# Attention's output projection moved into the steps, token selection into the last step, heavy path among light units

## What is computed

```python
q, k, v   = split((xn @ W_qkv + b_qkv).reshape(B, 16 heads, 1024, 48))
attention = softmax(q k^T * scale + causal mask) @ v, reshaped, @ W_out + b_out
light     = gelu(rms(xn) * gamma_l @ w1_l + b1_l) @ w2_l + b2_l        # hidden 128, all tokens
a, b      = 50 iterations of coordinate descent on s = xn @ routing_token
heavy     = for the 256 tokens of each batch with the largest exp((s + a + b) / 0.1):
            gelu(rms(xn) * gamma_h @ w1_h + b1_h) @ w2_h + b2_h        # hidden 1024
out       = x + attention + light + heavy (added to the rows of its tokens)
```

## Time and profile before

| | |
|---|---|
| time, median of 3 runs | 727.79 us (726.37 to 729.85) |
| the profiled execution, its own time | 727.58 us |
| its span, first to last instruction | 725.9 us |
| TensorE matmul busy | 673.3 us, 93% |
| VectorE busy | 552.7 us, 76% |
| ScalarE busy | 403.6 us, 56% |
| GpSimd busy | 380.2 us, 52% |
| mean granted TensorE clock | 0.983 |

### The profile page before, as it was taken

One profiled execution on the slowest core, in us unless ns is written; L12 is line 12 of the kernel. 1 busy time (PEld: TensorE's weight loads), 2 busy tenths in 40 slices (PEclk: granted clock), 3 DMA queues, 4 the chain that ended last, 5 costly groups with the idle time before them and its releaser, 6 DMA issues. The chain is left out here.

```text
span 725.9 us, 12455 instructions
## 1 busy us (share of the span) xinstructions
PE 673.3 (93%) x3987; PEld 295.4 (41%) x3987; DVE 552.7 (76%) x1565; ACT 403.6 (56%) x908; POOL 380.2 (52%) x774
## 2 busy tenths in 40 slices
PE   4977999899999997999999999999999999778996
PEld 2643545323333332333333333333333358664745
DVE  4854877899999999999999999999996324643301
ACT  2421221478787783876778777776776753222140
POOL 5678200358676877488677554355453332246203
PEclk9999999999999997999999999999999999999999
DMA  8999866469689589587993664653930515661112
GB/s 276 211 217 221 204 204 189 117 135 143 124 124 181 99 148 154 95 160 128 137 176 61 122 95 56 88 102 48 183 45 8 130 15 190 201 190 58 17 13 30
DMA packets 247057, 92.49 MB, mean 127 GB/s; under 512 B 212992, under 2 KB 232608, under 8 KB 243872
## 3 DMA queue, kind: packets, MB, share of 16 engines
q1 hardware_dynamic: 245456, 89.60, 61.6%
q0 software_dynamic: 1536, 2.10, 1.8%
HBM read 56.65 MB, written 35.01 MB: 126 GB/s over the span
## 5 line engine op out<-in xcount | busy, mean ns | idle before, releaser
L1252 DVE CUSTOM_DVE_ANT_0 ps<-ps,maskrow 128x640 f32<-128x640 f32 (+7 forms) x512 | 374.8, 780 | 26.0 <-PE ps L999 24.3
L871 ACT ACTIVATE strips<-ps 128x512 f32<-128x512 f32 (+1 forms) x608 | 311.2, 577 | 103.6 <-PE ps L1025 91.3
L999 PE MATMUL ps<-QTk,QTq 96*128 96x512 bf16 (+3 forms) x768 | 188.4, 336 | 18.4 <-DVE mx L1252 15.3
L1025 PE MATMUL ps<-QTq,QTk 99*128 99x512 bf16 (+3 forms) x768 | 185.1, 330 | 1.1 <-DMA QTq<-m_d 0.5
L1043 PE MATMUL ps<-strips,vext 128*32 128x512 f32 (+3 forms) x1536 | 162.2, 497 | 0.0
L999 PEld LDWEIGHTS ps<-QTk,QTq 96*128 96x128 bf16 x768 | 51.7, 98 | 173.0 <-DVE mx L1252 150.2
L1025 PEld LDWEIGHTS ps<-QTq,QTk 99*128 99x128 bf16 x768 | 67.6, 98 | 89.9 <-ACT strips L871 44.7
L967 PE MATMUL ps<-shared,xrT 128*128 128x384 f32 (+1 forms) x256 | 96.4, 510 | 5.1 <-DVE shared L1219 5.0
L1677 POOL TENSOR_SCALAR_AFFINE_SELECT strips<-strips 128x512 f32<-128x512 f32 x128 | 79.1, 634 | 36.9 <-ACT strips L871 36.4
L1252 DVE DVE_READ_ACCUMULATOR2_ANT mx<- 128x1 f32 x512 | 72.3, 141 | 0.0
L967 PEld LDWEIGHTS ps<-shared,xrT 128*128 128x128 f32 x256 | 48.0, 198 | 32.6 <-issue 9.3
(11 more groups left out here) (145 smaller groups left out, 680.4 us busy)
## 6 DMA issues: line engine op xcount, KB each, us to landing
qkv_d<-shared SPq DMA_DIRECT2D x32, 384.0 KB, 3.7
pieces_d<-pieces SPq DMA_DIRECT2D x64, 192.0 KB, 3.4
qk<-qkv_d SPq DMA_DIRECT2D x64, 128.0 KB, 3.9
QTq<-pieces_d SPq DMA_DIRECT2D x16, 384.0 KB, 5.1
QTk<-pieces_d SPq DMA_DIRECT2D x16, 384.0 KB, 7.6
vext<-qkv_d SPq DMA_DIRECT2D x16, 256.0 KB, 5.7
QTq<-pieces_d SPq DMA_DIRECT2D x16, 256.0 KB, 5.6
QTk<-pieces_d SPq DMA_DIRECT2D x16, 256.0 KB, 8.4
```

What stands on the lines that cost most here:

```text
L871: nc.scalar.activation(dst, src, ACT.Exp, scale=SCALE).then_inc(exp_done, 1)
L999: mm = pe.matmul(psM[:, s, at:at + n], QTq[0:W, f % 3, c * 1024 + qb * P:c * 1024 + (qb + 1) * P], QTk[0:W, f % 3, c * 1024 + k0:c * 1024 ...
L1025: mm = pe.matmul(psE[:, (NE * q + j) % ES, k * n:(k + 1) * n], QTk[0:W + 3, q % 3, c * 1024 + kb * P:c * 1024 + (kb + 1) * P], QTq[0:W + 3 ...
L1252: ins = nc.vector.tensor_tensor_reduce(scores, scores, maskrow[:, 1024 - n:1024], 1.0, MASKED, ALU.add, ALU.max, mx[:, f % 2, 8 * c + qb:8 ...
```

## The change

**Projection in the steps.** For steps 0 to 13 the attention output is projected two steps later. The E ring now also holds WT (behind E item 14) and WO (behind E item 20): SP loads the step's 256 tokens of sa_d into `sw`, TensorE transposes four blocks (WT), ScalarE copies them to `swT`, TensorE multiplies by wout (WO, four products of 256 columns), ScalarE copies to `att`, SP stores over the same rows of sa_d. In the tail the first seven units add the projected rows to x on VectorE (`sums`) and their tiles have one product left, the last unit (tokens of steps 14 and 15) still has three. **Selection.** TIES, SLOTS, HOT (16 pairs of one-hots), N (numbers of one batch) and G (gather of one batch) are items of the planner, placed from the keys on; their PSUM is a slot of `psM`. `xg`, `xgn` and `hot` lie in the buffers of the pieces. **Tail.** Both halves of the heavy path stand among the light units. `psH` has two banks instead of four. **Planner.** STEP, PACE, SOON, LATER, BEHIND and the time of the bulk load are other numbers.

The core of the diff:

```diff
 NE = len(EXPS)
+
+PROJECTED = STEPS - 2
+WT_AT, WO_AT = 14, 20
+RING = [x for q in range(STEPS) for j in range(NE)
+        for x in ([("E", q, j)] + ([("WT", q - 2)] if j == WT_AT and 2 <= q else []) + ([("WO", q - 2)] if j == WO_AT and 2 <= q else []))]
+RING_AT = {x: n for n, x in enumerate(RING)}
...
-STEP, PACE = 27.53, 31.86
-SOON, LATER, BEHIND = 0.19, 11.5, 1.84
+STEP, PACE = 29.03, 30.89
+SOON, LATER, BEHIND = 0.19, 14.1, 1.40
...
+            if kind in ("E", "WT", "WO"):
+                n = RING_AT[x] - ES
+                return latest(0.0 if n < 0 else after(("Scalar", RING[n])),
+                              done.get(("landed", ("LM", x[1]))) if kind == "E" else done.get(("landed", ("WL", x[1]))) if kind == "WT"
+                              else after(("Scalar", ("WT", x[1]))))
...
-        psS = ps[:, 2]
-        psH = ps[:, 2:6]
+        psH = ps[:, 2:4]
...
+        sw = osb[:, 0:512].rearrange("p (t e) -> p t e", e=E)
+        att = osb[:, 512:1024]
+        swT = xr[:, :, :].rearrange("p u e -> p (u e)")
+        pieces_free = pieces[:, :, :, :].rearrange("p b k n -> p (b k n)").bitcast(F32)
+        xg = pieces_free[:, 0:2048].rearrange("p (t e) -> p t e", e=E)
         xgT = QTk[:, 0, :].bitcast(F32).rearrange("p (k n) -> p k n", k=KE)
         saT = strips[:, 8192:8704].rearrange("p (b e) -> p b e", b=2)
-        hotb = strips[:, 0:4096].bitcast(BF16).rearrange("p (t n) -> p t n", n=NUM_HEAVY)
+        hot = [y.bitcast(BF16).rearrange("p (t n) -> p t n", n=NUM_HEAVY)
+               for y in (qk[:, :, :].rearrange("p b f -> p (b f)"), qkT[:, :])]
...
+            def load_outputs(q):
+
+                sp.wait_ge(sa_st[q % 2], 64 * (q // 2 + 1))
+                if q == 0:
+                    sp.wait_ge(smax_done, 1)
+                else:
+                    sp.wait_ge(qk_ps, RING_AT["WT", q - 1] + 1)
+                sp.dma_start(sw, sa2[q]).then_inc(sw_in, 16)
+
+            def store_projected(q):
+
+                sp.wait_ge(exp_done, RING_AT["WO", q] + 1)
+                sp.dma_start(sa2[q], att.rearrange("p (t e) -> p t e", e=E)).then_inc(att_st, 16)
...
+            def load_sa(i, u):
+
+                if 2 * i + u < NT // 4 - 1:
+                    sp.wait_ge(att_st, 16 * (4 * i + 2 * u + 2))
+                else:
+                    for p in range(2):
+                        sp.wait_ge(sa_st[p], 64 * (NQ // 2))
                 sp.dma_start(sa_in[:, u], sb3[bass.ds(2 * i + u, 1)].rearrange("a p t e -> (a p) t e")).then_inc(c_in[u], 16)
...
+            def outputs_over(q):
+
+                act.wait_ge(qk_ps, RING_AT["WT", q] + 1)
+                nc.scalar.activation(swT, psE[:, RING_AT["WT", q] % ES, :], ACT.Copy).then_inc(exp_done, 1)
+
+            def projected(q):
+
+                act.wait_ge(qk_ps, RING_AT["WO", q] + 1)
+                if q == 0:
+                    act.wait_ge(smax_done, 1)
+                else:
+                    act.wait_ge(att_st, 16 * q)
+                nc.scalar.activation(att, psE[:, RING_AT["WO", q] % ES, :], ACT.Copy).then_inc(exp_done, 1)
...
+            hidden(0, 0)
+            hidden(0, 1)
+            gathered(0)
+            heavy_hidden(0, range(4))
+            hidden(1, 0)
+            heavy_hidden(0, range(4, 6))
+            hidden(1, 1)
+            heavy_hidden(0, range(6, NHC))
+            hidden(2, 0)
+            act.wait_ge(gu_done, 2 * NSLOT + 1)
+            nc.scalar.activation(gscore[:, :], gu[:, :], ACT.Exp, scale=1.0 / EPS_ROUTE).then_inc(gs_done, 1)
+            hidden(2, 1)
+            gathered(1)
+            heavy_hidden(1, range(4))
+            hidden(3, 0)
+            heavy_hidden(1, range(4, 6))
+            hidden(3, 1)
+            heavy_hidden(1, range(6, NHC))
+            last_outputs()
 
...
+                elif kind == "TIES":
+                    pe.wait_ge(sl, 7)
+                    pe.wait_ge(consts, N_CONST)
+                    pe.matmul(psM[:, s, 0:2 * NT], ones[:, :], above[:, :, :].rearrange("p w n -> p (w n)"), start=True, stop=True)
+                    mm = prefix(psM[:, s, 2 * NT:3 * NT], above[:, 1, :])
+                elif kind == "SLOTS":
+                    so, to = place["TIES",]
+                    pe.wait_ge(free[so], to + 1)
+                    mm = prefix(psM[:, s, 0:NT], chosen[:, :])
+                elif kind == "N":
+                    b = item[1]
+                    pe.wait_ge(hot_done, 8 * (b + 1))
+                    for hh in range(2):
+                        for k in range(8):
+                            mm = pe.matmul(psM[:, s, 2 * hh:2 * hh + 2], hot[b % 2][:, k, hh * P:(hh + 1) * P],
+                                           tokid[:, :, 8 * b + k], start=(k == 0), stop=(k == 7))
...
+            def outputs_over(q):
+
+                n = RING_AT["WT", q]
+                pe.wait_ge(exp_done, n + 1 - ES)
+                pe.wait_ge(sw_in, 16 * (q + 1))
+                for t in range(2):
+                    for k in range(KE):
+                        at = (KE * t + k) * P
+                        mm = pe.transpose(psE[:, n % ES, at:at + P], sw[:, t, k * P:(k + 1) * P], ident[:, :])
+                mm.then_inc(qk_ps, 1)
+
+            def projected(q):
+
+                n = RING_AT["WO", q]
+                pe.wait_ge(exp_done, max(RING_AT["WT", q] + 1, n + 1 - ES))
+                if q == 0:
+                    pe.wait_ge(wout_in, 16)
+                for t in range(2):
+                    for k in range(KE):
+                        at = (KE * t + k) * P
+                        mm = pe.matmul(psE[:, n % ES, t * E:(t + 1) * E], swT[:, at:at + P], wout[:, k, :],
+                                       start=(k == 0), stop=(k == KE - 1))
+                mm.then_inc(qk_ps, 1)
+
...
+            def light_out(i, u, t, stop):
+
                 n = 8 * i + 4 * u + t
                 if t == 0:
+
+                    pe.wait_ge(h_done, 2 * i + u + 1)
+                if n >= 2:
+
+                    pe.wait_ge(ob_done, n - 1)
+                return pe.matmul(psC[:, t % 2, 0:E], hT[:, u, t * P:(t + 1) * P], w2l, start=True, stop=stop)
+
+            def unit(i, u):
+                for t in range(4):
...
+            def last_unit():
+
+                last_over(0)
                 for t in range(4):
                     if t < 3:
+                        last_over(t + 1)
+                    light_out(B - 1, 1, t, False)
+
+                    pe.wait_ge(saT_done, t + 1)
+                    for k in range(KE):
+                        mm = pe.matmul(psC[:, t % 2, 0:E], saT[:, t % 2, k * P:(k + 1) * P], wout[:, k, :],
+                                       start=False, stop=(k == KE - 1))
+                    mm.then_inc(o_ps, 1)
+
...
+            tail_open()
+            unit(0, 0)
+            unit(0, 1)
+            gathered(0)
+            heavy_hidden(0, range(4))
+            unit(1, 0)
+            heavy_hidden(0, range(4, 6))
+            unit(1, 1)
+            heavy_hidden(0, range(6, NHC))
+            unit(2, 0)
+            heavy_out(0, range(2))
+            unit(2, 1)
+            heavy_out(0, range(2, 4))
+            gathered(1)
+            heavy_hidden(1, range(4))
+            unit(3, 0)
+            heavy_hidden(1, range(4, NHC))
+            last_unit()
+            heavy_out(1, range(4))
...
+            def one_hots(j):
+
+                b = j // 4
+                if j == 0:
+                    dve.wait_ge(consts, N_CONST)
+
+                    dve.wait_ge(tp_done, NQ)
+                    dve.wait_ge(piece_done, 3 * NQ)
+                    s, at = place["SLOTS",]
+                    dve.wait_ge(free[s], at + 1)
+                if b >= 2 and j % 4 == 0:
+
+                    s, at = place["N", b - 2]
+                    dve.wait_ge(full[s], at + 1)
+                for k in (2 * j, 2 * j + 1):
+                    nc.vector.tensor_scalar(hot[b % 2][:, k % 8, :], iota256[:, :], slot[:, k:k + 1], None, ALU.is_equal
+                                            ).then_inc(hot_done, 1)
+
+            def rows_chosen(b):
+
+                s, at = place["N", b]
+                dve.wait_ge(full[s], at + 1)
+                ip = psM[:, s, 0:4].rearrange("p (h w) -> p h w", w=2)
+                nc.vector.tensor_scalar(idxf[:, 2 * b:2 * b + 2], ip[:, :, 0], float(P), None, ALU.mult).then_inc(idx_done, 1)
+                dve.wait_ge(idx_done, b + 1)
+                nc.vector.tensor_tensor(idx[:, 2 * b:2 * b + 2], idxf[:, 2 * b:2 * b + 2], ip[:, :, 1], ALU.add).then_inc(free[s], 1)
...
+                        if 2 * i + u < NT // 4 - 1:
+                            dve.wait_ge(c_in[u], 16 * (i + 1))
+                            nc.vector.tensor_tensor(x_in2[:, u], x_in2[:, u], sa_in[:, u], ALU.add).then_inc(sums, 1)
+                            dve.wait_ge(sums, 2 * i + u + 1)
...
             gathered_stats(0)
-            unit(B - 1, 1, range(2))
+            unit(0, 0)
             gathered_invert(0)
```

(36 more changed lines are left out.)

381 lines of the change are left out of this document (180 added, 201 removed).

## The result

The changed kernel took 741.06 us (median of 4 runs, 738.86 to 746.02) beside 728.17 for the kernel before: a ratio of 1.0187, 95% interval 1.0129 to 1.0244. The forecast was 722.8, its range 710 to 739. Both profiled executions compare by their spans, 725.9 and 737.1 us; the one of after is the fastest of its four runs (738.86 by its own time).

The account below looks back on a forecast made before the run. VectorE was taken to pace the steps, with slack in TensorE, and TensorE to bound the tail. Steps +7.0, last step +8.1 and tail -19.9 sum to -4.8, so 727.6 becomes 722.8 us; range 710 to 739.

Parts of the forecast that it names:

- The tail: Part behind the steps, walked through by each engine's written order: 114 us against 133.9, bounds 106 and 122.
- two clock dips: In the tail: TensorE's clock falls after idle time, counted twice at 1.7 us each.
- The steps: Projection work added to the steps: 31 us of TensorE time, of which 7 us lengthen them, bounds 0 and 31.
- the third: In the steps: share of added TensorE work passed on, judged by one slowed step's length; gives 10 us.
- the dip at 298 us: Slow TensorE clock from 280 to 290 us before the change; its step took 30.48 us, 1.65 over the mean.
- the seventh: In the steps: share of added TensorE work passed on, judged by VectorE's extra idle time; gives 4.5 us.
- The last step: From 555 us, TensorE without slack: 2.4 us of projection and 5.7 of selection count in full, +8.1 us.
- The rule for it: GpSimd additions and certain VectorE operations exclude each other; counted in the tail as half a collision, 1.2 us.
- The first rival: In the steps: TensorE becomes the bound; 736.5 us if two thirds of 31 pass on, 746.8 if all; chance 0.21.
- Selection late: Last step: routing ends late, TensorE stands with exponentials queued behind; costs 5 to 8 us, giving 729; chance 0.1.
- The port: Tail: each of six GpSimd additions holds a VectorE sum or normalisation for 2.36 us; 732.5 us; chance 0.06.
- The tail better than my walk: Tail: light units' stalls overlap with heavy work, so it nears 106 us and the time 714.8; chance 0.15.

Follow-up runs that it names:

- e6: Changed kernel with GpSimd's six additions of x placed behind its last gather; 742.25 us.
- e1: Changed kernel without the projection of steps 0 to 13, the first seven tail units adding unprojected outputs; 731.36 us.
- e4: Changed kernel with WT and WO each reduced to one bf16 product, ring slots, waits and copies kept, projection values left out; 740.83 us.
- e5: Changed kernel with WO's products issued twice; 770.37 us.
- e11: Changed kernel without the projection of steps 0 to 13 and with GpSimd's additions of x behind its last gather; 725.05 us.
- e8: Changed kernel with the tail in another order, same work, and GpSimd's additions of x behind its last gather; 728.33 us.
- e10: e8's tail order with the whole projection back in the tail, selection in the last step, the changed kernel's planner constants; 724.58 us.
- e3: Kernel before with the changed kernel's five planner constants and bulk load time, nothing else; 735.13 us.
- e9: e8's tail order with the whole projection back in the tail, selection in the last step, the old planner constants; 737.09 us.

## Why the prediction was wrong

Between the forecast of 722.8 and the profiled run's 738.86 lie 16.0 us: 8.9 in the last step, 5.5 in the steps, 1.3 ahead of them and 0.3 in the tail. The median is 2.2 higher still.

**The tail was right in its order, and its 114 was partly luck.** 114 was forecast and 114.2 measured, the first heavy product 16.3 us into it and measured 16.1. But the forecast had two clock dips of 1.7 us each. In this profile the clock stood at 1.2 GHz for 10.2 us from 628.8, then for 6.8 from 659.5; in e6, whose tail has the same order, for 17.1 from 624.9 and twice for 6.8, and that tail took 121.5. Tails in this same order took 120.6 to 121.9 us in e1, e4, e5, e6 and e11, each with 30.7 us at the low level, where the kernel after had 17.0. The profiled run of after is the fastest of four, so its tail is likely its shortest.

**The steps: +7.0 forecast, +12.5 measured.** The projection's share is 9.4 (against e1) or 8.9 (e8 against e10, e6 against e11), net of the clock dip that only the kernels without it have in full, within the bounds of 0 and 31 and near the third, 10, that the dip at 298 us had shown; the seventh, from VectorE's idle time in the dip, drew my value too low. WO and WT took 1.95 and 0.6 us, about the 2.4 of the forecast, so the price of the work was right and the part that passes on was too small. The other 3.0 us came from the planner's constants (e1 against before; 3.8 in e3, 2.9 in e10 against e9), which the forecast had listed as changed and given no term.

**The last step: +8.1 forecast, +17.0 measured.** This is the step that failed: both terms of its sum, 5.7 for the selection and 2.4 for the projection, were too small. The table of the runs splits the 17.0: 37.1 before, 44.6 with the selection and the new constants (e11), 52.6 with the projection (e6), 54.1 with the additions beside the one-hots (after). So the selection with the constants cost 7.5, the projection 8.0 and the lock 1.5.

The selection was 5.7 us of TensorE's work with VectorE's side "at nothing". Its rows (two passes of 1.7 us in the fence below, the numbers and the small products) add to 6.7 in e11 and after, and the new constants gave 1.1 in e3: with the additions out of the way, VectorE's side was indeed at nothing. Beside them it was 1.5 (after against e6) or 3.1 (e1 against e11, part of it clock). The rule for it was in the forecast, with the pair of the earlier trace rows, but was applied to the sums in the tail alone; the one-hots that I moved to stand beside the same additions were the very operation of that row. The Trainium skill, "SBUF — State Buffer", section "SBUF: two separate sides", counts among the VectorE operations that such an addition locks out those in a two-port mode as well as those with two SBUF inputs. The trace agrees as far as the lock goes (4 one-hots in 1.13 us alone, in 3.17 beside an addition of 2.38); no run here shows which mode a one-hot, with one SBUF input, was in.

The projection in this piece was one WT and WO, 2.4 us. It cost 8.0 (e6 against e11) or 8.1 (e8 against e10). TensorE's groups in the last piece (mean ns of one behind the busy time), kernel after, then e10, then the kernel before:

```profile
L1198 PE MATMUL ps<-strips,vext 128*32 128x512 f32 (+3 forms) x168 | 17.1, 496 | 0.0
L1156 PE MATMUL ps<-QTq,QTk 99*128 99x512 bf16 (+3 forms) x71 | 16.2, 327 | 0.0
L1121 PE MATMUL ps<-xrT,w1l 128*128 128x512 f32 x32 | 15.3, 601 | 0.0
L1181 PE MATMUL ps<-shared,xr 128*128 128x256 f32 x16 | 3.9, 385 | 0.0
L1093 PE MATMUL ps<-above,ones 128*128 128x28 f32 (+6 forms) x14 | 1.7, 262 | 0.0
L1093 PE MATMUL ps<-chosen,ones 128*128 128x28 f32 (+6 forms) x14 | 1.7, 262 | 0.0
...
L1169 PE MATMUL ps<-ident,osb 128*128 128x128 f32 x4 | 0.6, 272 | 0.0
```

```profile
L1201 PE MATMUL ps<-strips,vext 128*32 128x512 f32 (+3 forms) x160 | 16.8, 507 | 0.5 <-POOL strips L1861 0.5
L1159 PE MATMUL ps<-QTq,QTk 99*128 99x512 bf16 (+3 forms) x63 | 13.5, 320 | 0.0
L1124 PE MATMUL ps<-xrT,w1l 128*128 128x512 f32 x27 | 12.9, 599 | 0.0
```

```profile
L1006 PE MATMUL ps<-xrT,w1l 128*128 128x512 f32 x32 | 15.2, 595 | 0.0
L1043 PE MATMUL ps<-strips,vext 128*32 128x512 f32 (+3 forms) x140 | 14.1, 492 | 0.0
L1025 PE MATMUL ps<-QTq,QTk 99*128 99x512 bf16 (+3 forms) x60 | 12.5, 317 | 0.0
```

When the last maxima end, the kernel after has two WO still to do, not one (3.9 and 0.6 for one WT), and 8 score products, 8 PV records (four products) and 5 light records more than e10: 2.7, 0.3 and 2.4 us. Together 9.9, of which some overlaps, for 8.0 or 8.1 in the last piece; e6 and e8 show the same counts as the kernel after. Against the kernel before, the kernel after has 3.7 us more of scores, 3.0 of PV, 4.5 of WO and WT and 6.7 of selection: 17.9 for the 17.0. So the projection had delayed the other work in the steps without delaying the maxima by as much, and the debt fell due where nothing covers it. A pace measured from maxima to maxima misses that.

**The trade.** The forecast weighed 7 + 2.4 us of projection in front of T against about 30 leaving the tail. Measured it is 17 to 18 in front of T (e8 against e10, e6 against e11). The first rival, TensorE as the bound of the steps, named the point where this decides, with the forecast's last step and tail: 11.8 us for the steps. It came to 12.5 there and 17.0 in the last step, so the sign was that rival's; its picture, VectorE waiting for TensorE in the steps, was not, for those waits rose only from 10.5 to 18.9. e5 shows what it would look like: 41.9.

**Selection late** did not come as described: TensorE stood 1.09 us ahead of one group of slot products and 1.20 ahead of another, not 5 to 8. **The port** is real and stood elsewhere. **The tail better than my walk** needed another order: e8's is 103.0.

What stays open: how the projection's 17 to 18 us divide between TensorE's work and the ring slots with their copies. e4 takes 5.1 of 9.4 us in the steps away and leaves 4.3, but it leaves some of TensorE's work too; for the last piece the run was disturbed. No run cuts WO into smaller pieces or moves it elsewhere in the ring, so whether it would then fit into the waits is open as well.

## What to carry to other kernels

Waits that sum to a large number are not room for work: divide them by their count, and compare that with the piece that is to go in. When work is put ahead of a point where one engine becomes the bound, count that engine's backlog at that point (items begun late but not yet done) and not the pace up to it alone. When a step moves to another place, look up what runs on the other engines there, and retune a planner's constants with the move: the same five numbers cost 6 us in one order and saved 12 in another.

## What was not expected of the hardware

TensorE's clock fell behind pauses of TensorE, and the work behind the pause then paid for it too. Windows of the kernel after, ahead of and in each fall:

```profile
622.90:628.80 5.90, 2.17 (x8) 1.25 (x8) 5.19 (x14) 0.10 (x1) 3.21 (x4) 0.99 0.38 46
...
628.80:639.00 10.20, 6.08 (x17) 3.81 (x16) 6.67 (x21) 1.53 (x4) 4.31 (x9) 0.51 0.61 190
...
649.00:659.50 10.50, 5.56 (x16) 2.74 (x16) 8.78 (x32) 1.98 (x3) 4.95 (x6) 0.99 0.49 150
...
659.50:666.30 6.80, 4.40 (x8) 2.56 (x9) 4.58 (x8) 0.00 (x0) 0.73 (x1) 0.51 0.14 47
```

TensorE was busy 2.17 of 5.9 us ahead of the first fall and 5.56 of 10.5 ahead of the second; then it ran at the 1.2 GHz level for 10.2 and 6.8 us, and what took 6.08 and 4.40 us of busy time there would have taken about half at the upper level: by these rows some 3.0 and 2.2 us lost, an estimate. In e10, whose tail keeps TensorE busy 108.5 of 119.5 us, the clock fell nowhere between 602 us and the last products. In e8, whose tail holds less work and more idle time, it was at the low level for 17.0 us. So work taken out of a stretch where other engines then can't keep up is partly paid back in clock.
